# A two-layer graph network on one core: three kept partial sums are added by VectorE instead of TensorE, and a tile of codes is made one step earlier

## The reference

```python
def _ggc(x, adj, W, wih, whh, bih, bhh):
    m = adj @ (x @ W)
    gi = m @ wih.T + bih
    gh = x @ whh.T + bhh
    ...
    r = sigmoid(i_r + h_r); z = sigmoid(i_z + h_z); n = tanh(i_n + r * h_n)
    return (1.0 - z) * n + z * x
h = relu(_ggc(x, adj, W1, ...));  x1 = layernorm(x + relu(_ggc(h, adj, W2, ...)))
# layer 1
rank = cumsum(adj != 0, axis=1); deg = rank[:, -1:]; k = minimum(deg, 100)
pos = rank - (deg - k)
w = mask * where(pos > 0, 0.5 ** (k - pos), 0.0)
out = layernorm(x1 + w @ (x1 @ weight) + bias)
```

## Time and profile before

| | |
|---|---|
| median of 3 runs | 345.53 us (345.31 to 345.88) |
| profiled execution, its own time | 346.18 us |
| span of the profiled execution | 344.1 us |
| TensorE busy | 328.7 us, 96% |
| VectorE busy | 299.2 us, 87% |
| ScalarE busy | 187.6 us, 55% |
| GpSimd busy | 47.2 us, 14% |
| mean granted TensorE clock | 0.998 |

### The profile page before, as it was taken

One profiled execution on the slowest core, in us unless ns is written; L12 is line 12 of the kernel. 1 busy time (PEld: TensorE's weight loads), 2 busy tenths in 40 slices (PEclk: granted clock), 3 DMA queues, 4 the chain that ended last, 5 costly groups with the idle time before them and its releaser, 6 DMA issues.

```text
span 344.1 us, 6780 instructions
## 1 busy us (share of the span) xinstructions
PE 328.7 (96%) x2540; PEld 154.0 (45%) x2540; DVE 299.2 (87%) x494; ACT 187.6 (55%) x245; POOL 47.2 (14%) x50
## 2 busy tenths in 40 slices
PE   1998999999999999999999999999999999999993
PEld 0442334333333333333333333546364544789993
DVE  0689879899999999997999678878999999968996
ACT  0203304105122047068467437897977869768995
POOL 2000000000000000000000001250514232233275
PEclk9999999999999999999999999999999999999999
DMA  6999999999999998999898999998999996000003
GB/s 240 414 410 409 410 407 410 404 402 367 399 396 370 366 392 327 351 360 352 291 336 301 378 368 381 392 344 324 339 379 391 346 381 249 4 16 4 2 2 123
DMA packets 32143, 107.85 MB, mean 313 GB/s; under 512 B 3568, under 2 KB 6512, under 8 KB 32112
## 3 DMA queue, kind: packets, MB, share of 16 engines
q1 hardware_dynamic: 31248, 106.15, 81.4%
q10 hardware_dynamic: 864, 1.28, 1.1%
HBM read 106.37 MB, written 1.05 MB: 312 GB/s over the span
## 4 chain that ended last, share of the span: by engine, by line
PE 78%; DMA 10%; DVE 8%; issue 2%; POOL 0%; ACT 0%; POOLq 0%; ACTq 0%; DVEq 0%; SPq 0%
PE m_acc L509 41%; PE out L509 17%; DMA stream<-in_adj_t 9%; PE out L647 8%; PE gate_ps L585 4%; DVE codes L1241 3%; PE gate_ps L592 3%; PE m_acc L647 2%; DMA w<-in_w 2%; PE gate_ps L609 1%; PE gate_ps L614 1%; DVE s_in L1298 1%; DVE codes L1052 1%; DVE stream L1305 1%; PE m_acc L556 1%
## 5 line engine op out<-in xcount | busy, mean ns | idle before, releaser
L509 PE MATMUL m_acc<-stream,s_in 128*64 128x512 f32 x488 | 119.1, 596 | 1.2 <-DMA stream<-in_adj_t 0.9
L1052 DVE TENSOR_SCALAR codes<-stream 128x1024 uint8<-128x1024 f32 x109 | 71.8, 686 | 6.4 <-DMA stream<-in_adj_t 6.2
L509 PE MATMUL out<-stream,s_mid 128*64 128x512 f32 x264 | 66.3, 593 | 0.0
L968 POOL TENSOR_TENSOR rstd<-stat,mhalf 128x4 f32<-128x4 f32 (+1 forms) x17 | 25.6, 1510 | 277.2 <-DVE stat L1207 277.1
L509 PEld LDWEIGHTS m_acc<-stream,s_in 128*64 128x64 f32 x488 | 32.8, 136 | 63.7 <-issue 48.4
L509 PE MATMUL m_acc<-stream,s_mid 128*64 128x512 f32 x224 | 51.8, 600 | 0.2 <-DMA stream<-in_adj_t 0.2
L1101 DVE SCALAR_TENSOR_TENSOR codes<-codes,run 128x384 uint32<-128x384 uint32 (+2 forms) x62 | 45.4, 732 | 2.1
L1096 DVE TENSOR_TENSOR run<-run,codes 128x768 uint16<-128x768 uint16 (+2 forms) x61 | 43.6, 715 | 2.0
L745 ACT ACTIVATE m_high<-m_acc 64x512 f32<-64x512 f32 x13 | 7.7, 594 | 56.3 <-PE m_acc L509 47.7
L842 ACT ACTIVATE wexp<-codes,code_bias 128x2048 uint16<-128x2048 uint8 x18 | 35.7, 1992 | 0.1
L509 PEld LDWEIGHTS out<-stream,s_mid 128*64 128x64 f32 x264 | 18.9, 137 | 37.1 <-issue 36.4
(11 more groups left out here) (179 smaller groups left out, 413.4 us busy)
## 6 DMA issues: line engine op xcount, KB each, us to landing
stream<-in_adj_t SPq DMA_DIRECT2D x192, 512.0 KB, 6.1
wexp<-in_adj_t SPq DMA_DIRECT2D x2, 512.0 KB, 5.5
late<-in_adj_t SPq DMA_DIRECT2D x2, 512.0 KB, 6.6
third<-in_x_pairs SPq DMA_DIRECT2D x8, 128.0 KB, 6.2
out_nodes<-stream SPq DMA_DIRECT2D x7, 128.0 KB, 2.0
hx<-in_x_pairs ACTq DMA_DIRECT2D x1, 512.0 KB, 7.1
third<-in_adj_t SPq DMA_DIRECT2D x1, 512.0 KB, 8.0
run<-in_adj_t SPq DMA_DIRECT2D x1, 512.0 KB, 9.5
```

Of the source, the lines that this page charges most:

```text
L509: last = nc.tensor.matmul(to[D * u:D * (u + 1), :], state[:, t * D:(t + 1) * D], data[:, u * CW:(u + 1) * CW], start=start[u], stop=stop)
L968: nc.gpsimd.tensor_tensor(rstd[:, r, nodes], stat[:, r, nodes], mhalf[:, nodes], ALU.pow).then_inc(rstd_made, 1)
L1052: nc.vector.tensor_scalar(edges(p // 2, b, 2 * (p % 2), 2), loaded(n), 0.0, None, ALU.not_equal).then_inc(mask_made, 1)
```

## The change

The kept sums of product steps 11, 12 and 15 (`WITH_KEPT`) no longer enter through TensorE. In steps 3, 4 and 7 VectorE adds accumulator's upper half and kept sum into `m_high` (`high_kept`), between residual and combining, and ScalarE's copy of that half goes. The kept sums of product steps 13 and 14 stay with TensorE. One tile of codes goes from step 3 to step 2. Blocks expanded into the place "k" wait also for the new add that reads it.

```diff
+WITH_KEPT = (NCH + 3, NCH + 4, 2 * NCH - 1)
...
-CHAIN = [chain_tiles(*x) for x in ((0, 6), (6, 12), (12, 16), (16, 21), (21, 25), (25, 29), (29, 32),
+CHAIN = [chain_tiles(*x) for x in ((0, 6), (6, 12), (12, 17), (17, 21), (21, 25), (25, 29), (29, 32),
...
-                if first and ch in KEPT:
+                if first and ch in KEPT and g not in WITH_KEPT:
...
+                if PLACE[j, i] == "k":
+                    act.wait_ge(high_copied, NCH + 5)
...
-                    high(g + 1)
+                    if g + 1 not in WITH_KEPT:
+                        high(g + 1)
...
+            def high_kept(g):
+                _, _, part = kept_part(2 * NCH - 1 - g)
+                dve.wait_ge(pair_used, USED[g])
+                dve.wait_ge(m2_kept, len(KEPT))
+                dve.wait_ge(m_ready, g)
+                nc.vector.tensor_tensor(m_high[0:D, :], acc_bank(g)[D:P, :], part, ALU.add)\
+                    .then_inc(high_copied, 1)
...
+                if g + 1 in WITH_KEPT:
+                    high_kept(g + 1)
                 if t < NCH:
                     combine(g + 1)
```

More of the change, by code:

```diff
@@ L1240, in expand @@
                     dve.wait_ge(h_made, NCH + 4)
+                if PLACE[j, i] == "k":
+                    dve.wait_ge(high_copied, NCH + 5)
                 nc.vector.tensor_scalar(weights(j, i).bitcast(U16), block(j, i), float(P),
```

## The result

The changed kernel takes 348.00 us (median of 4 runs, 347.41 to 348.55) against 345.54 us (345.31 to 345.88) of the kernel before, run beside it: ratio 1.0067, 95% interval 1.005 to 1.0084, slower by 2.46 us. The forecast was 347.2 with a range of 344.9 to 347.8. Its sign and its mechanism held; two terms of its sum were too small and one was missing.

The account below looks back on a forecast made before the run. TensorE and VectorE were taken as both full in steps 3 to 6. Line 1128's delay went +0.38, +0.27, +1.11, then +1.68 us with the adds and step 7's slack: 345.53 + 1.68 = 347.2 us, range 344.9 to 347.8.

Parts of the forecast that it names:

- TensorE's relief: Three kept sums leave TensorE, 0.58 us each; 1.16 us remain and are used up in steps 4 to 6, waiting for VectorE.
- The moved tile: Step 3 to step 2: relief mostly idle time before ScalarE; a rival had it pay for the adds, 345.5 us, chance 0.18.
- The 0.27 us of slack in step 7: Step 7, ScalarE: the sigmoid could have begun at 306.00 and did at 306.27, so 1.95 us of lateness becomes 1.68.
- the last stretch: From 315 us on: neither TensorE nor VectorE has slack, so everything shifts by 1.68 us.
- the first term of the sum: End of step 2, VectorE: the moved tile's 2.39 us go into 2.06 us of idle time, delaying line 1128 by 0.38 us.
- the upper edge of its range: Forecast's own upper end: the moved tile may take 0.35 us longer, as in step 3, making 347.6 us.
- The add: Steps 3, 4 and 7, VectorE: each new add costs 0.84 us, 0.12 + 0.72, with 0.60 as the other end.
- Step 6: Steps 5 and 6 have neither an add nor idle time and carry the +1.11 us on unchanged.
- Rival C: Steps 5 and 6: ScalarE's expanded weights also come late for TensorE, adding at most one more add, 348.0 us; chance 0.05.
- The first kept sum: Step 2, TensorE: its 0.58 us saving buys nothing, since TensorE then waits longer for a tile of the adjacency matrix.
- The load wait that should have grown to 0.78 us: TensorE at 214.67: a 0.20 us wait for an adjacency matrix tile, expected to become 0.78 us.

Follow-up runs that it names:

- experiment 3: Changed kernel with TensorE also still adding the three kept sums, so they are added twice: 347.71 us, ratio 1.0063.
- experiment 6: Changed kernel with one of ScalarE's two expands ahead of step 4's sigmoid moved into its wait for line 1226: 346.25 us, ratio 1.001.
- Experiment 4: Changed kernel with GpSimd's bias add of step 2 cut to a quarter of its elements: 347.46 us, ratio 1.0046.
- experiment 8: Changed kernel with each new VectorE add reading the lower 64 partitions instead of the upper 64: 347.20 us in one run.
- the fastest kernel: Changed kernel with ScalarE's expand moved earlier in step 3, no add in step 7 and step 7's expand before its exponential: 345.11 us, ratio 0.9985.
- the undisturbed before: The kernel before, unedited, profiled a second time, with no load wait at the first kept sum: 345.11 us.

## Why the prediction fell short

**What held.** VectorE pays, and with its idle time filled TensorE's relief is worth nothing (experiment 3). The moved tile does not pay, because ScalarE's fixed order holds step 4's sigmoid 4.11 us behind its conversion of line 1226's result (245.91 to 250.02, forecast 4.11); experiment 6 shows it by taking one expand away. The 0.27 us of slack in step 7 are there, as 0.29: line 1226 shifts by +2.27 (304.89 + 0.44 - 303.06) and step 8 by +1.98. GpSimd, SP and the last stretch add nothing: it is full, and the end has step 8's shift within 0.03 us.

**The step that failed** is the first term of the sum, "2.39 us of work go into 2.06 us of idle time, and +0.38 us comes out". The idle time was right: in the other trace of before it is 2.02 us, with the whole step 0.42 us earlier. The work was not: the tile's first instruction took 1.63 us and not 1.21, so the term is 0.81 us (+0.39 and -0.42 in the table), 0.43 more than forecast. The prediction had seen this kind of slowness (1.57 us in step 3) and put 0.35 us on top as the upper edge of its range. But it took the tile's price from 236.65, where GpSimd has nothing to do, and did not ask what GpSimd does at its new place. The trace of before shows it, in a row that the prediction did not read:

```profile
229.04 2.77 POOL L977 TENSOR_TENSOR s_in<-late,third 128x256 f32<-128x256 f32 x1
```

It ends at 231.81, 0.58 us behind the maximum (231.23), right where the tile was to start. Experiment 4 gives 0.40 us back.

**The add** costs 0.90 us and not 0.84: three times 0.06 is 0.18 us. The 0.12 us ahead of it were right, and experiment 8 shows that they come from the upper partitions. What follows it was taken from a row where the next instruction does not use its result: 0.72 us; here it does, 0.78.

**Step 6** lost 0.12 us that no term had. From residual to combining add it takes 0.46 us there (285.62 to 286.08), 0.34 before. It is so in all kernels with an add in step 4, not in the others. It is also there with adds in the lower partitions. Its cause stays open.

**Rival C** named 348.0, the time that was measured, but its course is not what happened. TensorE did wait for ScalarE's weights in steps 5 and 6, 0.52 us each. These waits never reach VectorE, whose rows show no idle time from 250.50 to step 7. And the fastest kernel has neither of these waits, while its step 6 loses the 0.12 us all the same.

**The sum** with the measured terms, against the undisturbed before: 1.68 + 0.43 + 0.18 + 0.12 = 2.41 us, where the traces give 2.35 and the medians 2.46 and 2.15. The forecast is thus short by 0.5 to 0.8 us, of which the tile is the largest part; the second median of the changed kernel, 347.78, lies just inside the stated range.

**The first kept sum** was rightly put at nothing, for a wrong reason. The load wait that should have grown to 0.78 us is missing in eight of the twelve traces, and the waits at this place make at most 0.41 us together where a kernel has the relief. The saving is lost 5 us later, in 0.54 us of waiting for GpSimd's support (line 986), which hangs on VectorE and not on TensorE.

**Where a better kernel lies.** The adds of steps 3 and 4 can be borne when ScalarE's expand moves up (experiment 6), since VectorE then keeps what the moved tile leaves it. The add of step 7 can't: it lies on the path to the end, and leaving it out, with ScalarE's expand of step 7 moved up, gives 0.81 us back in the traces (+0.04 to -0.77) and 1.14 in the medians. What remains as a gain over the kernel before is 0.4 to 0.5 us.

## What to carry to other kernels

When an instruction is moved into idle time, price it at the place where it goes: look at what GpSimd does in those microseconds, and ask which fixed order on a third engine stands between the place it left and the next thing that counts. Taking work from the busiest engine gave nothing here where its results met an engine without idle time, and 0.78 us where that engine had some; when two engines are full in the same stretch, ask at each step which of them is last. Before a term of a few tenths is built on one wait in one trace, see it in a second trace.

## What the runs showed of the hardware

VectorE and GpSimd took turns where they met. GpSimd's bias add spanned 2.77 us but ended 0.58 us behind VectorE's 2.65-us maximum; a quarter of it ended 0.17 us behind. rstd on 128x4 numbers took 1.02 us with VectorE idle and 1.93 beside a VectorE expand of 1.21. The bias add took 0.72 us with VectorE idle. VectorE's 128x2048 uint16 operation, 1.21 to 1.23 us alone, took 1.63 behind the bias add. A long span on GpSimd's row can so be waiting, and it is worth looking at what VectorE does beside it.

An instruction of VectorE that reads its PSUM operand from the upper 64 partitions started 0.11 us later than the same one in the lower 64. An add whose result the next instruction reads held the engine for 0.76 to 0.79 us, where the combining add in front of an unrelated instruction holds it for 0.60.
